# The front stage of an AdaLN attention and mixture-of-experts block: a contiguous inverse, column groups for the small projections, and u and o in 512 columns

## The reference, cut to what matters

```
attn = -(kb @ k^T), strictly lower            # per chunk and head, 32x32
for i in 1..31: attn[i, :i] += attn[i] @ attn[:, :i]
attn = attn + I                               # the inverse that is applied below
u, w = attn @ v, attn @ kb
step:  u_new = u_i - w_i @ S
       o_i   = q_i @ S + attn_local @ u_new   # attn_local = masked q_i k_i^T
       S     = S + k_i^T @ u_new
beta = sigmoid(hs @ Wb); floor = sigmoid(hs @ floor_W + b); fus = gelu(hs @ W1 + b1) @ W2 + b2
q, k normalised by sqrt(sum of squares per head)
```

## Time and profile before

| | |
|---|---|
| median of 3 runs | 1125.28 us (1121.94 to 1126.48) |
| the profiled execution | 1122.48 us, its span 1120.8 us, so 1.7 us lie around the span |
| instructions in the span | 40853, of which TensorE 36514 (matmuls and weight loads) |
| TensorE (PE) busy | 835.6 us, 75% |
| VectorE (DVE) busy | 739.5 us, 66% |
| ScalarE (ACT) busy | 452.6 us, 40% |
| granted TensorE clock, mean | 0.87 |
| front stage, recurrence with projections (rounds 1 to 10) | 201.02 to 528.25 us |
| front stage, recurrence without projections (rounds 11 to 15) | 528.25 to 645.4 us |

### The profile page before, as it was taken

The page is one execution under the profiler, slowest core; times in us unless marked ns, Lnnn a source line. Parts: engine busy times, 40 slices in busy tenths (PEclk is TensorE's granted clock), DMA queues, the critical chain, the costliest instruction groups (busy, mean ns, idle before and its releaser), DMA issues. The chain is left out here.

```text
span 1120.8 us, 40853 instructions
## 1 busy us (share of the span) xinstructions
PE 835.6 (75%) x18257; PEld 523.6 (47%) x18257; DVE 739.5 (66%) x1589; ACT 452.6 (40%) x864; POOL 203.2 (18%) x227
## 2 busy tenths in 40 slices
PE   1389987999999999999655665979877246666660
PEld 1134444665566566656545663545432023454440
DVE  3133998888988888898877138998986524232320
ACT  1577664565655554554210112567575111001000
POOL 2000000000000000000000000111111057888875
PEclk9999998999999999999776776989897569778775
DMA  5210111111100101110000074344352124344432
GB/s 121 50 33 25 35 35 36 36 37 46 35 34 27 37 27 37 37 37 23 28 13 13 13 210 157 99 124 116 97 131 57 27 80 92 69 70 82 73 36 25
DMA packets 86439, 66.12 MB, mean 59 GB/s; under 512 B 18504, under 2 KB 72952, under 8 KB 86264
## 3 DMA queue, kind: packets, MB, share of 16 engines
q1 hardware_dynamic: 73580, 54.42, 17.3%
q0 software_dynamic: 11264, 8.40, 5.6%
q10 hardware_dynamic: 1420, 0.70, 0.2%
HBM read 36.33 MB, written 27.15 MB: 57 GB/s over the span
## 5 line engine op out<-in xcount | busy, mean ns | idle before, releaser
L576 PE MATMUL ps_p<-f_hT,Wconv 128*128 128x512 f32 x384 | 188.5, 620 | 1.6 <-ACT f_hT L546 1.6
L670 DVE TENSOR_TENSOR f_L<-f_L,f_prod 128x60 f32<-128x60 f32 (+14 forms) x240 | 121.2, 505 | 8.3
L667 DVE TENSOR_TENSOR f_prod<-f_L 128x60 f32<-128x60 f32 (+14 forms) x240 | 118.8, 495 | 6.0
L1286 POOL DMA_INDIRECT out_dram<-y,slot_row x64 | 101.2, 1582 | 28.3 <-issue 18.3
L576 PEld LDWEIGHTS ps_p<-f_hT,Wconv 128*128 128x128 f32 x384 | 67.7, 191 | 68.3 <-issue 61.5
L1335 ACT ACTIVATE act_g<-pe_g 128x512 f32<-128x512 f32 x32 | 17.4, 594 | 167.0 <-PE pe_g L1313 140.4
L427 POOL COPY f_v_pad<-f_v_pad 128x32 f32<-128x32 f32 x15 | 5.6, 373 | 419.7 <-ACT f_v_pad L509 419.7
L556 PE MATMUL ps_a<-f_TT,f_r 32*32 32x64 f32 x2048 | 60.4, 283 | 27.7 <-DVE f_L L716 17.1
L1303 PE MATMUL pe_x<-ident,got 128*128 128x128 f32 x64 | 15.6, 389 | 87.6 <-DMA got<-xh_dram,slot_row 87.6
L556 PEld LDWEIGHTS ps_a<-f_TT,f_r 32*32 32x32 f32 x2048 | 56.0, 129 | 37.5 <-issue 26.5
L1277 POOL DMA_INDIRECT got<-xh_dram,slot_row x64 | 62.4, 974 | 58.6 <-POOLq L1166 39.4
(11 more groups left out here) (238 smaller groups left out, 1801.1 us busy)
## 6 DMA issues: line engine op xcount, KB each, us to landing
w<-in_L_ffn_w_dram SPq DMA_DIRECT2D x48, 128.0 KB
f_x_in<-_attn_hidden_states_dram SPq DMA_DIRECT2D x16, 256.0 KB, 2.9
s_tok_dram<-f_s_tok SPq DMA_DIRECT2D x16, 256.0 KB, 2.0
o_tok_dram<-f_o_tok SPq DMA_DIRECT2D x16, 256.0 KB, 2.0
b_s_in<-s_tok_dram SPq DMA_DIRECT2D x16, 256.0 KB, 2.9
b_o_in<-o_tok_dram SPq DMA_DIRECT2D x16, 256.0 KB, 3.0
b_x_in<-_attn_hidden_states_dram SPq DMA_DIRECT2D x64, 64.0 KB, 2.0
out_dram<-b_x SPq DMA_DIRECT2D x64, 64.0 KB, 1.8
```

The lines of the kernel that those rows point to most:

```text
L576: last = pe.matmul(ps[:, :], g.Wconv[:, which, tap, :], tokens(t, tap), start=(tap == 0), stop=(tap == TAPS - 1))
L667: dve.tensor_tensor(tmp, M[:, :, m + 1:, m:m + 1].broadcast_to([P, 2, rows, cols]), M[:, :, m:m + 1, 0:cols].broadcast_to([P, 2, rows, col ...
L670: dve.tensor_tensor(M[:, :, m + 1:, 0:cols], M[:, :, m + 1:, 0:cols], tmp, ALU.add).then_inc(s["solved"], 1)
L1286: pool.indirect_dma_start(flat_out, bass.IndirectOffsetOnAxis(ap=g.slot_row[:, t, n:n + 1], axis=0), y[t % 2][:, n * D:(n + 1) * D], None, ...
```

## The change

Four things are done at once.

1. u and o are made 512 columns wide. The stationary operand is `r_apart` or `u_apart`, `[P, G2, NB, C]`: for each of the two heads of a quad a copy in which the other head's channels are zero (zeroed once by GpSimd; afterwards only the own half is written). `two_heads` issues two 32-column matmuls per sequence and quad and accumulates them. The part q @ S of o (L625 before) needs no copies and becomes 32 columns wide. VectorE's two transposes are now 512 wide, the one of o goes straight to `o_tok`, ScalarE's `take_valid` for o is gone and that for u is one pass over 512 elements.
2. The inverse TT is stored as `[NB, C, G2]`; the moving operand of u reads it with a step of 2, and VectorE's transpose writes it with that step. D_T falls from 4 to 2.
3. `sm` becomes `dense`: five matmuls with 32-column stationary operands, each of four groups in a quad of output partitions of its own, a copy to SBUF by ScalarE, and one matmul with the 0/1 table `spread`, which puts each row in its place. That matmul stands behind r in the next round, and so do VectorE's transpose of sm and all that follows from it.
4. The order is moved: u and o are split in two halves around a projection, ScalarE takes v earlier, VectorE transposes k and v earlier and o last.

The core of the diff:

```
-D_K, D_Q, D_KT, D_W, D_KG, D_T, D_A = 3, 6, 6, 5, 5, 4, 4
+D_K, D_Q, D_KT, D_W, D_KG, D_T, D_A = 3, 6, 6, 5, 5, 2, 4
-        TT_all = k.sb("f_TT", [P, D_T, C, NI])
+        TT_all = k.sb("f_TT", [P, D_T, NB, C, G2])
+        r_apart, u_apart = k.sb("f_r_apart", [P, G2, NB, C]), k.sb("f_u_apart", [P, G2, NB, C])
+            def two_heads(out, lhs, rhs, first, last, start):
+                for b in range(first, last):
+                    for n2 in range(G2):
+                        for q in range(NQ):
+                            ins = pe.matmul(out[quad(q), b * C:b * C + C], lhs[quad(q), n2, b, :], rhs(b, n2, q),
+                                            start=(start and n2 == 0), stop=(n2 == 1), skip_group_check=True)
+                return ins
+                inverse = lambda b, n2, q: TT[d % D_T][quad(q), b, :, n2]
+                masked = lambda b, n2, q: attn[d % D_A][quad(q), 2 * b + n2, :]
...
+                if t4 is not None:
+                    ps = free_bank(pe, "sm", t4)
+                    need(pe, s["dense_ready"], t4)
+                    pe.matmul(ps[:, :], g.spread[:, :], dense[:, :], start=True, stop=True).then_inc(s["sm_ps"], 1)
...
-                    per_pair(double(ps_a), narrow(r), lambda b, q: TT[d % D_T][quad(q), :, 2 * b:2 * b + 2].rearrange("p i g -> p g i"), every)\
-                        .then_inc(s["u_ps"], 1)
+                    two_heads(ps_a, r_apart, inverse, 0, NB // 2, True)
                 if t is not None:
                     project(t, "v", 2, 0)
+                if d is not None:
+                    two_heads(ps_a, r_apart, inverse, NB // 2, NB, True).then_inc(s["u_ps"], 1)
...
-                    per_pair(double(ps_b), narrow(state[(d - 1) % 2]),
-                             lambda b, q: q_cm[d % D_Q][quad(q), b * C:b * C + C].unsqueeze(1).broadcast_to([32, G2, C]), in_bank, stop=False)\
-                        .then_inc(s["o1_ps"], 1)
+                    per_pair(narrow(ps_b), narrow(state[(d - 1) % 2]), narrow(q_cm[d % D_Q]), at_first, stop=False).then_inc(s["o1_ps"], 1)
...
-                    per_pair(double(ps_b), narrow(u_tok), lambda b, q: attn[d % D_A][quad(q), 2 * b:2 * b + 2, :].rearrange("p g c -> p (g c)"), never)\
-                        .then_inc(s["o_ps"], 1)
+                    two_heads(ps_b, u_apart, masked, 0, NB // 2, False)
+                if t is not None:
+                    ps = free_bank(pe, "f1", t)
+                    pe.matmul(ps[:, :], g.fus_W1[:, P:2 * P], tokens(t, TAPS - 1), start=True, stop=True).then_inc(s["f1_ps"], 1)
+                if d is not None:
+                    two_heads(ps_b, u_apart, masked, NB // 2, NB, False).then_inc(s["o_ps"], 1)
...
-                    pe.matmul(ps[:, :], g.small_w[:, 2, :], tokens(t, TAPS - 1), start=True, stop=False)
+                    pe.matmul(ps[quad(1), :], g.small_w[:, 2, :], tokens(t, TAPS - 1), start=True, stop=True)
                     need(pe, s["square_k"], t)
-                    pe.matmul(ps[:, :], g.small_w[:, 3, :], square[0][:, :], start=False, stop=False)
+                    pe.matmul(ps[quad(2), :], g.small_w[:, 3, :], square[0][:, :], start=True, stop=True)
...
-                    dve.tensor_tensor(r[:, :], ps_r[:, :], w_tok[d % D_W][:, :], ALU.subtract).then_inc(s["r_ready"], 1)
+                    dve.tensor_tensor(own_half(r_apart), halves(ps_r), halves(w_tok[d % D_W]), ALU.subtract).then_inc(s["r_ready"], 1)
...
-                    dve.transpose(u_wide[:, :], ps_a[:, :]).then_inc(s["u_ready"], 1)
+                    dve.transpose(u_tok[:, :], ps_a[:, 0:W]).then_inc(s["u_ready"], 1)
...
-                    dve.transpose(o_wide[:, :], ps_b[:, :]).then_inc(s["o_turned"], 1)
+                    dve.transpose(o_tok[d % 2][:, :], ps_b[:, 0:W]).then_inc(s["o_turned"], 1)
...
-                    take_valid(u_tok, u_wide).then_inc(s["u_copied"], 1)
+                    act.activation(own_half(u_apart), halves(u_tok), ACT.Copy).then_inc(s["u_copied"], 1)
...
+                    need(act, s["dense_ps"], t)
+                    act.activation(dense[:, :], ps_p[bank["dense", t]][:, :], ACT.Copy).then_inc(s["dense_ready"], 1)
```

More of the change, by code:

```diff
@@ L233, in _ @@
             dve.memset(g.full_s[:, :], float(S)).then_inc(full_ready, 1)
-            then(dve.memset(band[:, :], 0.0), dve.memset(g.small_w[:, :, :], 0.0))
+            then(dve.memset(band[:, :], 0.0), dve.memset(g.small_w[:, :, :], 0.0), dve.memset(g.spread[:, :], 0.0))
             dve.wait_ge(mod_ready, 1)
@@ L306, in stage_front @@
         square = [k.sb(f"f_square{n}", [P, W]) for n in "kq"]
+        dense = k.sb("f_dense", [P, W])
         hid = [k.sb(f"f_hid{m}", [P, W]) for m in range(2)]
@@ L355, in stage_front @@
         for i in range(FIRST, NCH):
-            for kind, n in [(x, unit(i + 5)) for x in ("k", "v", "q", "f0", "f1")] + [("x", unit(i + 9)), ("sm", unit(i + 5))]:
+            for kind, n in [("sm", unit(i + 4))] + [(x, unit(i + 5)) for x in ("k", "v", "q", "f0", "f1")] + [("x", unit(i + 9)), ("dense", unit(i + 5))]:
                 if n is not None:
@@ L533, in _ @@
                     upper_to_identity(L[t3 // 2 % 2][:, t3 % 2, :, :]).then_inc(s["L_masked"], 1)
[L534 to L538, removed]
                 if n is not None:
                     need(act, s["x_ps"], n)
-                    need(act, s["sm_ps"], 4 * (n // 4) - 5)
+                    need(act, s["dense_ps"], 4 * (n // 4) - 5)
                     need(act, s["halo_ready"], n - 4)
@@ L548, in _ @@
                     last.then_inc(s["h_ready"], 1)
+                if t is not None:
+                    need(act, s["dense_ps"], t)
+                    need(act, s["sm_ps"], t - 1)
+                    act.activation(dense[:, :], ps_p[bank["dense", t]][:, :], ACT.Copy).then_inc(s["dense_ready"], 1)
         @block.tensor
@@ L736, in _ @@
                     dve.transpose(kg_cm[t4 % D_KG][:, :], kg_tok[:, :]).then_inc(s["kg_ready"], 1)
+                part(0, 3)
                 if d is not None:
@@ L740, in _ @@
                     need(dve, s["u_copied"], d - 1)
-                    need(dve, s["o_copied"], d - 1)
-                    dve.transpose(u_wide[:, :], ps_a[:, :]).then_inc(s["u_ready"], 1)
-                part(0, 3)
+                    dve.transpose(u_tok[:, :], ps_a[:, 0:W]).then_inc(s["u_ready"], 1)
+                if t is not None:
+                    need(dve, s["silu_k"], t)
+                    need(dve, s["s_ps"], t - D_KT)
+                    dve.transpose(k_tok[t % D_KT][:, :], k_cm[t % D_K][:, :]).then_inc(s["k_turned"], 1)
+                part(3, 5)
+                if t is not None:
+                    need(dve, s["silu_v"], t)
+                    if t >= 6:
+                        dve.wait_ge(v_out[t % 2], 16 * ((t - 3) // 2 if t % 2 else (t - 4) // 2))
+                    need(dve, s["w_ready"], t - 2)
+                    dve.transpose(by_seq(v_of(t)), v_pad[t % 2][:, :, FIR_S - 1:]).then_inc(s["v_turned"], 1)
+                part(5, 6)
                 if t3 is not None:
```

157 lines of the change are left out of this document (73 added, 84 removed).

## The result

The changed kernel takes 1188.46 us, median of 4 runs (1183.78 to 1191.15), against 1125.88 us for the kernel before beside it (4 runs, 1121.94 to 1132.76): a ratio of 1.055 [1.051, 1.059]. It is slower by 5.5%, and the forecast of 1177 us with its range of 1140 to 1214 holds. The profiled execution took 1191.15 us.

A forecast was written before the change was run, and what follows sets the result against it. The prediction took TensorE's instruction supply, 3.77 us per packet of 256, as the bound. Its terms, 24.9 + 29.9 - 2 - 1.5 + 0.5 = +51.8 us, led to 1177 us, with a range of 1140 to 1214.

The forecast's parts named there:

- The supply of instructions is the bound: Rounds 1 to 15: TensorE waits for its instructions, which come in packets of 256, at 3.77 us each; chance 0.77.
- The signs that the forecast named: Rounds 1 to 10 take 35 us each, rounds 13 to 15 take 26 each, VectorE idles 7 us a round.
- TensorE's work shrinks: Rounds 1 to 10: narrower u and q @ S and dense cut PE's 32.1 us a round to about 29.2.
- Rounds 1 to 10: Packets grow from 73.2 to 93.4 and the supply comes latest: +24.9 us, bounds -3.1 and +50.1.
- 352.1 us at 3.77 us a packet: Rounds 1 to 10: time that 93.4 packets need, against 327.2 us before.
- Nearly everywhere it asks quicker than 3.77, so the supply never rests for long: Rounds 1 to 10: PE between wide matmuls would need 3.1 us for about 132 records, 2.2 in masked @ u's halves.
- Rounds 11 to 15: Packets grow from 29.0 to 39.0, 147.0 us at 3.77 each: +29.9 us, bounds +18.2 and +40.4.
- Round 0: Wait for VectorE's solve unchanged; behind it 6.3 packets take 24 us instead of 26.2: -2 us.
- The terms at nothing: ScalarE's passes, VectorE's step-of-2 transpose (at most +1.2 us a round, covered) and the later L: nothing or nearly; setup +0.5 us.
- 1 (supply hidden): Rounds 1 to 15: instructions come fast enough, so TensorE's savings count: 1086 us, chance 0.05.
- 2 (quicker beside wide matmuls): Rounds 1 to 10: packets take some 3.1 us, behind them 3.77: 1123 us, chance 0.06.
- 3: Rounds 1 to 10: gaps lower PE's clock to 0.74, its work takes 39.5 us a round: 1220 us, chance 0.12.

The follow-up runs named there:

- e5: The changed kernel with 12 more wide matmuls a round in rounds 12 to 15, two behind each of six small blocks; 1191.84 us.
- e3: The changed kernel with 60 of the 64 state-update matmuls left out from round 1 on; 1144.87 us.
- e4: The kernel before with 60 of the 64 state-update matmuls left out from round 1 on; 1112.50 us.
- e7: e1 with 128 one-column matmuls added to each round, half ahead of r and half ahead of u; 1223.24 us.
- e1: The changed kernel with u and o as pairs of heads again, inverse layout, dense and spread kept; 1104.95 us.
- the three doses: e1, the changed kernel with only o as pairs again (1133.88 us), and the changed kernel: 7.3, 8.3 and 9.3 packets a round in rounds 1 to 10.
- e2: The kernel before with only the inverse stored as [sequence, column, head], so u reads it with a step of 2; 1114.03 us.
- e8: e1 with attn and u_pick in bfloat16, so masked @ u needs one matmul instruction and one weight load instead of two; 1093.26 us.

## Why the prediction was right, step by step

- **The supply of instructions is the bound.** Shown: by the gaps that come every 256 instructions, by 34 us of added TensorE work that cost 5.6 (e5), by one block being worth 35.7 us in the changed kernel's rounds 1 to 15 and 8.5 in those before (e3, e4), and by nearly empty matmuls that cost as much as the real ones behind round 10 (e7). The signs that the forecast named came: 36.0 us a round for 35, 26.5 in rounds 13 to 15 for 26, and VectorE idle for 7.9 us a round for 7.
- **TensorE's work shrinks.** Half of u takes 1.21 us as forecast, and `dense` 1.86 (308.43 to 310.29) for the 2.1 assumed. The useful parts are worth 20 us by themselves (e1), and the doubling turns them into a loss of 63.
- **The sum.** The span of the profiled execution grew by 68.2 us, 16.4 more than forecast: 7.5 in round 0, 8.3 in rounds 1 to 10 and 4.3 of scatter, less 3.1 and 0.6 in the other two rows.
- **Rounds 1 to 10: +33.2 for +24.9.** The mechanism was right, the term "352.1 us at 3.77 us a packet" was too small: the 93.3 packets took 3.86 each. 3.77 had been read where nothing else was late; here six waits for L add 1.7 us (93.3 packets at 3.77 and these make 353.4, so 7 us are left that no single wait explains), and the three doses show that one bound takes over from the other only by degrees. "Nearly everywhere it asks quicker than 3.77, so the supply never rests for long" was the step that took this for nothing.
- **Rounds 11 to 15: +26.8 for +29.9.** 39.0 packets took 3.69 us each over the part, 3.84 in its last 50 us. The term was a little too large.
- **Round 0: +5.5 for -2.** This step failed, in two places. First, I had the wait for L end no later. Counted from r of round 0 it ends 20.0 us in (156.59 to 176.58) for 16.7 before (158.16 to 174.81): +3.3. TensorE arrives 1.6 us earlier, and L comes 1.8 us later. TensorE's r, before and after, and VectorE, before and after:

```profile
158.16 1.29 PE L556 MATMUL ps_r<-f_state,f_kg_cm 32*32 32x32 f32 x128
156.59 1.29 PE L561 MATMUL ps_r<-f_state,f_kg_cm 32*32 32x32 f32 x128
```

```profile
169.28 0.65 DVE L688 TENSOR_TENSOR f_r<-ps_r,f_w_tok 128x512 f32<-128x512 f32 x1
...
173.46 1.21 DVE L716 STREAM_TRANSPOSE f_L<-ps_a 128x1024 f32<-128x1024 f32 x1
```

```profile
157.77 1.22 DVE L782 TENSOR_TENSOR f_attn<-ps_b,causal 128x1024 f32<-128x1024 f32 x1
...
170.32 0.65 DVE L707 TENSOR_TENSOR f_r_apart<-ps_r,f_w_tok 128x512 f32<-128x512 f32 x1
170.90 0.70 DVE L713 STREAM_TRANSPOSE f_sm_tok<-ps_p 128x512 f32<-128x512 f32 x1
...
175.22 1.21 DVE L737 STREAM_TRANSPOSE f_L<-ps_a 128x1024 f32<-128x1024 f32 x1
```

  Only 0.7 of the 1.8 us lies between r and L, where sm's transpose now stands; it stood ahead of r before. The other 1.0 is there already when r starts, and in that part VectorE now has the masked copy of `ps_b` (L782, 1.22 us), which it had done by 152.5 us before.

  Second, I priced the burst behind the wait by the supply alone, 6.3 packets in 24 us. TensorE's own work there is more than that, 25.45 us, at a granted clock of 0.87, and two gaps add 2.8 us: 28.4 for 26.2 before. The packet in stock was there. The burst in two parts, up to its first gap and behind it, and TensorE's timeline:

```profile
176.58:195.00 18.42, 18.18 (x718) 11.37 (x719) 15.85 (x41) 9.25 (x16) 0.48 (x2) 0.89 0.14 46
195.00:204.97 9.97, 7.27 (x213) 3.35 (x212) 6.12 (x10) 3.21 (x11) 0.00 (x0) 0.83 0.08 30
```

```profile
176.58 1.93 PE L575 MATMUL ps_a<-f_TT,f_r_apart 32*32 32x32 f32 x128 [12.08 <-DVE f_L L737]
178.44 3.05 PE L585 MATMUL ps_p<-f_hT,Wconv 128*128 128x512 f32 x4
...
196.17 0.78 PE L575 MATMUL ps_b<-f_attn,f_u_apart 32*32 32x32 f32 x68 [1.26 <-issue]
...
200.17 0.79 PE L575 MATMUL ps_b<-f_attn,f_u_apart 32*32 32x32 f32 x70 [1.53 <-issue]
```

  Up to 195.0 TensorE took 5.6 packets' worth in 18.4 us without a stop, 3.3 us each, where the pace of the late rounds would have brought 4.8.

- **The terms at nothing** held: VectorE's transpose of the inverse takes 1206 ns with its step of 2 (e2), and up to round 0 the change brought 1.6 us for the 1.0 forecast, which the scatter of single executions there does not let one confirm.
- **The rivals.** 1 (supply hidden) and 2 (quicker beside wide matmuls) fall with 360.4 us. 3 is half seen: the clock did fall, to 0.98 in rounds 1 to 10 and 0.56 in rounds 11 to 15, but it did not set the time: in rounds 1 to 10 it was near its upper level, far from the 0.74 that this rival wanted, and in the late rounds e5 shows it, with 0.92 from round 12 on and no gain. The rule that a block boundary is "mostly hidden" (the Trainium skill, "Runtime: NRT & Kernel Launch", section "Instruction fetch mechanics") describes e1's and the earlier kernel's rounds 1 to 10; for streams of small matmuls no run here agrees with it.

What bounds rounds 1 to 10 of e1 and e8 is not one thing. In e1 TensorE is busy 294.1 and VectorE 288.5 of 314.6 us; TensorE waits 11.9 us for VectorE and 6.3 for instructions. In e8 it is busy 281.6 of 311.3 us and waits 20.6 for VectorE and 6.8 for instructions. The share of the moved order is not separated from that of `dense`.
